# Taking a pacing wait off the slot scatters on GpSimd

## The chip, the cores and the metric

The program runs on 1 core of one Trainium2 chip. The metric is the device time of one execution in microseconds. Before the change it is 4115.81 us, the median of 3 executions (4109.86 to 4130.47).

## The reference

A block of a graph network with three parts. Node features are 6250 x 256, in float32; there are 200,000 edges sorted by target node.

```python
xn = _layernorm(x, axis=-1)
x = x + gnn(xn, ..., src, dst) + linear_attention(xn[None])[0]
x = x + moe(_layernorm(x, axis=-1)[None])[0]
# gnn: gather per edge by src, a small MLP per edge, segment_sum by dst, two linear maps
# moe, for 8 experts of 256 -> 1024 -> 256:
probs = softmax(xt @ Wr + br); top_p, top_idx = top_k(probs, 2)
weights = top_p / top_p.sum()
y = experts(xt)                       # every token
out = (weights * y[top_idx]).sum()    # two experts of 8 per token
```

The kernel computes only the two chosen experts of each token. For that it must sort tokens by expert: each token gets two slots in a table, one in the region of each of its experts.

## The kernel before, in words

The program has stages one after the other. The times are from the start of the profiled execution.

- **Prepare and nodes** (to about 350 us): layer norm, the node tables, attention sums.
- **Edges** (to about 3110 us): per item of four pieces of 128 edges, GpSimd (POOL) issues four indirect gathers (L812), TensorE (PE) computes edge weights (L953, L959), VectorE (DVE) and ScalarE (ACT) build messages, PE sums them by target (L972), and DVE adds the sums to accumulators (L870).
- **Update** (about 3122 to 3395 us), the stage of the change: 49 tiles of 128 tokens.
- **Experts** (from about 3395 us): blocks of 512 or 256 slots. POOL gathers token rows through the slot table and scatters weighted results.

In the update stage a step `s` handles several tiles at once, in a software pipeline. PE turns the sums of tile s+1 (L1200), makes the attention denominators of s+2 and s+1 (L1212, L1216), turns tile s-1 (L1238), makes the output of tile s (L1225, L1229) and the router logits of s-1 (L1244). DVE adds the residual and so completes a tile of `x2` (L1370, `onto_residual`), and computes statistics, shares and denominators (L1355, L1359, L1365). ACT copies results out of PSUM (L1297, L1303, L1310). SyncE (SP) loads residuals and queries three and four tiles ahead and stores tokens. The semaphore `c["x2"]` counts completed tiles.

Routing is done in batches of tiles, `SIZES = [8, 8, 8, 8, 8, 3, 3, 3]`; `done_at[b]` is the step at which batch b is complete. DVE runs one part of it in each of the steps `done_at[b]` to `done_at[b] + 4`: moments, best expert, next expert, weights, places. The first part hands two numbers per token to POOL for a power of -1/2 (`powers`, L1172), and the second waits for it. The last part, `places`, ends in `c["placed"]` (L1446), which says that the slot number of each token of the batch is known.

POOL then writes the slot table. `scatter(b, j)` issues two indirect DMAs (L1181), one for each chosen expert of the 128 tokens of tile j of the batch. Each writes 128 rows of 8 bytes to DRAM. A batch of eight thus has 16 of them. Each `scatter` waits for `placed`, and also for a count of `x2` that goes up by one per j (L1178). POOL's code is written out by a plain loop over steps, so between `scatter(b, 4)` and `scatter(b, 5)` stands `powers(b + 1)`. For batches 5 to 7 the work of several batches is interleaved.

At the end of the stage SP waits until all 98 scatters have landed and then loads the first rows of the slot table for the experts.

Of the kernel before, what the change touches and what calls it, by code (L numbers as in the profile page):

```python
# [21 lines left out]
NT = -(-N_NODES // P)  # L22
# [985 lines left out]
def update(nc, A, K, acc, out):  # L1008

    with ExitStack() as ctx:  # L1010
# [39 lines left out]
        c = {z: m.sem(z) for z in (  # L1050
            "ctxT", "ctxT_copied", "folded", "fold", "columns", "centred", "mid", "turned", "midT", "den", "positive", "inverse", "by_head", "share",
            "out", "x2", "passed", "stats", "x2_turned", "xT", "logits", "raw", "spread", "powers", "runner_up", "exp", "scales",
            "upto", "ranked", "counted", "placed", "known", "tok", "begun", "pads", "pads_out", "made")}
# [6 lines left out]
        done_at = [FIRSTS[b] + SIZES[b] for b in range(NB_R)]  # L1060
# [88 lines left out]
        @block.gpsimd  # L1149
        def _(pool):  # L1150
            g = nc.gpsimd
            g.iota(pads[:, :, 0], [[1, 512]], base=N_PAD, channel_multiplier=0)
            g.memset(pads[:, :, 1], 0).then_inc(c["pads"], 1)
            g.iota(ramp[:, :, :], [[0, MOST], [-1, E]], base=E, channel_multiplier=0, allow_small_or_imprecise_dtypes=True)
            g.iota(rows[:, :, :, 0], [[0, TOP], [P, NT]], base=0, channel_multiplier=1)
            g.iota(hot[0][:, :, 0:1], [[CAP // P, E]], base=0, channel_multiplier=0, allow_small_or_imprecise_dtypes=True)
            g.iota(origin[:, :], [[CAP, E]], base=0, channel_multiplier=0, allow_small_or_imprecise_dtypes=True)
            g.iota(number[:, 0:NDUO], [[1, NDUO]], base=0, channel_multiplier=0, allow_small_or_imprecise_dtypes=True)
            g.iota(number[:, NDUO:NBK], [[1, NSOLO // 2], [0, 2]], base=NDUO, channel_multiplier=0,
                   allow_small_or_imprecise_dtypes=True)  # L1160
            g.iota(number[:, NBK:], [[1, NSOLO]], base=0, channel_multiplier=0, allow_small_or_imprecise_dtypes=True)
            g.iota(ahead[:, 0:NDUO], [[2 * SB, NDUO]], base=0, channel_multiplier=0, allow_small_or_imprecise_dtypes=True)
            g.iota(ahead[:, NDUO:], [[2 * SB, NSOLO // 2], [SB, 2]], base=2 * SB * NDUO, channel_multiplier=0,
                   allow_small_or_imprecise_dtypes=True)
            g.memset(mask[:, :, :], 1.0).then_inc(c["made"], 1)
            pool.wait_ge(c["made"], 1)
            g.memset(mask[:, :, 0:1], 0.0).then_inc(c["made"], 1)
            pool.wait_ge(c["pads_out"], 16)

            def powers(b):  # L1170
                pool.wait_ge(c["spread"], b + 1)
                g.tensor_tensor(power[:, :, of(b)], power[:, :, of(b)],  # L1172
                                K.minus_half[:, 0:size(b)].unsqueeze(1).to_broadcast([P, 2, size(b)]),
                                ALU.pow).then_inc(c["powers"], 1)

            def scatter(b, j):
                pool.wait_ge(c["placed"], b + 1)
                pool.wait_ge(c["x2"], min(done_at[b] + 4 + j, NT))  # L1178
                for i in range(TOP):
                    z = TOP * FIRSTS[b] + i * SIZES[b] + j  # L1180
                    g.indirect_dma_start(out=K.slots_d, out_offset=bass.IndirectOffsetOnAxis(ap=where_i[:, z:z + 1], axis=0),  # L1181
                                         in_=rows[:, i, FIRSTS[b] + j, :], in_offset=None, bounds_check=NROW - 1, oob_is_err=True).then_inc(scattered, 16)

            for s in range(end_step + MOST):
                for b in range(NB_R):
                    if s == done_at[b]:
                        powers(b)
                    if 0 <= s - done_at[b] - 4 < SIZES[b]:
                        scatter(b, s - done_at[b] - 4)
# [767 lines left out]
```

## Time and profile before

| what | value |
|---|---|
| median of 3 executions | 4115.81 us |
| the profiled execution | 4115.81 us |
| its span, first to last instruction | 4114.1 us |
| mean granted TensorE clock | 0.935 of full |
| busy: PE / DVE / ACT / POOL | 85% / 65% / 64% / 57% of the span |

The profiled execution is the median one, and 1.7 us of it lie outside its span. An engine's busy time leaves out its waits. The busy shares are means over stages with different limits, so they say little about the update stage, which is 7% of the span.

### The profile page before, as it was taken

The page shows a single profiled execution, that of the slowest core. Times are in us where ns is not written, and L with a number is a line of the kernel's source. Part 1 is how long each engine was busy: PE and PEld are TensorE (multiplying, and loading weights), DVE is VectorE, ACT ScalarE, POOL GpSimd, SP SyncE. Part 2 cuts the span into 40 slices and gives each one's busy share as a digit, 9 for nine tenths or more (in the row PEclk, how much of TensorE's full clock was granted, in tenths as well). Part 3 has the DMA queues.
Part 4 walks back from the last instruction along what each step waited for, and adds up shares of the span by engine and source line. Part 5 has one row for each costly group of instructions (what it writes and reads, how often), then busy time and mean ns, then how long its engine had stood idle before and what let it go on. Part 6 is the DMA issues. An engine that isn't in the chain of part 4 may idle for free. (4 is left out here: it accounts for less than half of the span.)

```text
span 4114.1 us, 68468 instructions
## 1 busy us (share of the span) xinstructions
PE 3510.4 (85%) x16169; PEld 2945.0 (72%) x16169; DVE 2667.4 (65%) x4940; ACT 2635.5 (64%) x8253; POOL 2355.2 (57%) x2141
## 2 busy tenths in 40 slices
PE   6978888888988888888888888888888958999998
PEld 5867677676766776676676767677667847888887
DVE  7857677666767666676666767667785545565541
ACT  6666676666666666666666766666664536667652
POOL 6646666655656665666666666665641554445442
PEclk9989999999999999999999999999899979999999
DMA  7843233323323333333332333333323654454444
GB/s 233 276 152 88 83 86 89 87 80 84 90 82 90 84 86 82 85 90 85 86 86 82 91 88 85 87 86 84 85 70 91 117 117 125 127 148 126 131 116 131
DMA packets 321360, 431.06 MB, mean 105 GB/s; under 512 B 128875, under 2 KB 249143, under 8 KB 313079
## 3 DMA queue, kind: packets, MB, share of 16 engines
q0 software_dynamic: 105936, 253.72, 23.3%
q1 hardware_dynamic: 215335, 176.28, 14.8%
q8 instruction: 41, 0.67, 0.1%
q14 instruction: 48, 0.39, 0.0%
HBM read 365.18 MB, written 64.59 MB: 104 GB/s over the span
## 5 line engine op out<-in xcount | busy, mean ns | idle before, releaser
L812 POOL DMA_INDIRECT k_x<-gather_table,edges_edge x1612 | 1759.3, 1091 | 1075.9 <-issue 727.4
L831 ACT ACTIVATE k_x<-k_x,edges_edge 128x64 f32<-128x64 f32 x4836 | 1196.5, 334 | 28.9 <-DVE k_x L904 13.5
L959 PE MATMUL edges_ps_edge<-k_w_e,edges_hT 100*128 100x256 f32 x3224 | 851.7, 411 | 309.3 <-issue 155.5
L972 PE MATMUL edges_ps_sum<-k_x,edges_hot_y 128*128 128x256 f32 x3224 | 1003.6, 393 | 127.2 <-issue 75.9
L972 PE MATMUL edges_ps_sum<-k_x 128*128 128x256 f32 x3224 | 985.1, 387 | 11.4 <-issue 11.4
L959 PEld LDWEIGHTS edges_ps_edge<-k_w_e,edges_hT 100*128 100x128 f32 x3224 | 647.6, 205 | 458.5 <-issue 282.6
L841 ACT ACTIVATE edges_hot_y<-k_x,edges_edge 128x128 f32<-128x128 f32 x1612 | 516.7, 390 | 502.6 <-remote 346.8
L972 PEld LDWEIGHTS edges_ps_sum<-k_x,edges_hot_y 128*128 128x128 f32 x3224 | 624.7, 197 | 281.4 <-issue 152.5
L972 PEld LDWEIGHTS edges_ps_sum<-k_x 128*128 128x128 f32 x3224 | 629.9, 195 | 110.1 <-issue 18.5
L870 DVE TENSOR_TENSOR accumulators<-accumulators,edges_ps_sum 128x512 f32 x477 | 325.9, 683 | 431.8 <-remote 338.9
L904 DVE TENSOR_TENSOR k_x<-k_x,edges_ps_edge 128x512 f32<-128x512 f32 x403 | 275.7, 684 | 398.0 <-remote 320.3
L823 ACT ACTIVATE edges_hT<-edges_ps_hidden 100x512 f32<-100x512 f32 x403 | 237.7, 590 | 409.0 <-remote 296.3
L888 DVE TENSOR_TENSOR k_w_kvT<-k_x,edges_edge 128x768 f32<-128x768 f32 x403 | 384.4, 954 | 16.9 <-DMA k_x<-gather_table,edges_edge 16.8
L907 DVE TENSOR_TENSOR k_x<-k_x,edges_ps_edge 128x768 f32<-128x768 f32 x403 | 381.7, 947 | 0.0
L1763 ACT ACTIVATE experts_g<-experts_ps_h,weights_constants 128x512 f32<-128x512 f32 (+1 forms) x256 | 162.8, 638 | 246.5 <-PE experts_ps_h L1690 240.6
L879 DVE SCALAR_TENSOR_TENSOR k_x<-k_iota_f,k_item_base,edges_edge 128x512 f32<-128x512 f32 (+2 forms) x477 | 314.1, 663 | 1.9 <-issue 1.6
L1638 POOL DMA_INDIRECT out<-experts_y,weights_rows x112 | 198.0, 1768 | 167.1 <-issue 87.6
L1800 DVE TENSOR_TENSOR experts_g_lo<-experts_g,experts_g_hi 128x512 fp32r<-128x512 f32 x192 | 132.4, 690 | 227.4 <-ACT experts_g_hi L1763 227.4
L953 PE MATMUL edges_ps_hidden<-edges_el,k_w_e1s 128*100 128x512 f32 x403 | 253.5, 629 | 16.4 <-DMA edges_el<-el_parts 15.9
L1628 POOL DMA_INDIRECT k_x<-tokens,weights_rows x112 | 125.5, 1120 | 239.7 <-DMA weights_rows<-slots 186.7
L898 DVE TENSOR_TENSOR k_x<-k_w_kvT 128x256 f32<-128x256 f32 x403 | 171.1, 425 | 12.1
L894 DVE TENSOR_TENSOR k_w_kvT<-k_w_kvT 128x256 f32<-128x256 f32 x403 | 168.4, 418 | 0.0
(308 smaller groups left out, 4456.1 us busy)
## 6 DMA issues: line engine op xcount, KB each, us to landing
k_x<-in_w SPq DMA_DIRECT2D x64, 1024.0 KB
k_x<-gather_table,edges_edge POOLq DMA_INDIRECT x1612
el_parts<-nodes_el_parts SPq DMA_DIRECT2D x41, 384.0 KB
edges_el<-el_parts SPq DMA_DIRECT2D x355, 40.0 KB
edges_el<-el_parts SPq DMA_DIRECT2D x425, 20.0 KB
nodes_el<-in_el SPq DMA_DIRECT2D x41, 192.0 KB
k_x<-in_x SPq DMA_DIRECT2D x7, 896.0 KB
residual<-nodes_res SPq DMA_DIRECT2D x49, 128.0 KB
```

What stands on the lines that cost most here:

```text
L812: nc.gpsimd.indirect_dma_start(out=rows[k][:, j, :], out_offset=None, in_=K.table_d.rearrange("t p d -> (t p) d"), in_offset=bass.Indirect ...
L823: nc.scalar.activation(hT[k % 2][:, :], ps_h[k % 2][0:HID, :], ACT.Silu, scale=1 / math.sqrt(BAS)).then_inc(c["act"], 1)
L831: x = nc.scalar.activation(g[:, j, D + MUL * (i + 1):D + MUL * (i + 2)], g[:, j, 2 * D:MSG], ACT.Identity, scale=y[k][:, j, 1 + i:2 + i])
L841: x = nc.scalar.activation(hot_y[k % 2][:, j, :], hot[k][:, j, :], ACT.Identity, scale=y[k][:, j, 0:1])
L870: v.tensor_tensor(a, a, ps_s[ph.bank(k, j)][:, :], ALU.add).then_inc(c["flushed"], 1)
L879: v.scalar_tensor_tensor(hot[k][:, at, :], K.iota_f[:, :].unsqueeze(1).to_broadcast([P, ph.len, P]), K.item_base[:, bass.ds(ph.seq(n) + j, ...
L888: v.tensor_tensor(dot3[:, :, :, :], rows[k][:, :, MUL:D].rearrange("p c (i u) -> p c i u", i=3), y[k][:, :, 1:4].unsqueeze(3).to_broadcast ...
L904: v.tensor_tensor(g.rearrange("p c (b u) -> p c b u", u=MUL)[:, :, 0:MSG // MUL:8, :], f[:, :, 0:MUL].unsqueeze(2).to_broadcast([P, GC, 2, ...
L907: v.tensor_tensor(g[:, :, MUL:D].rearrange("p c (i u) -> p c i u", i=3), f[:, :, MUL:D].rearrange("p c (i u) -> p c i u", i=3), w[:, :, 1: ...
L953: t.matmul(ps_h[k % 2][0:HID, :], K.w_e1s[:, :], el[k][:, :], start=True, stop=True).then_inc(c["hidden"], 1)
L959: x = t.matmul(ps_e[k % 2][:, j * 256:(j + 1) * 256], hT[k % 2][:, j * P:(j + 1) * P], K.w_e2[:, :], start=True, stop=True)
L972: x = t.matmul(into[:, :, o, :], rows_hot[:, j, :], msg[k % 2][:, j, o * D:(o + 1) * D], start=j % ph.len == 0 and o == 0, stop=(j + 1) % ...
```

## The change

One wait is deleted from `scatter`. After it, a scatter waits for `placed` of its batch alone.

```diff
             def scatter(b, j):
                 pool.wait_ge(c["placed"], b + 1)
-                pool.wait_ge(c["x2"], min(done_at[b] + 4 + j, NT))
                 for i in range(TOP):
                     z = TOP * FIRSTS[b] + i * SIZES[b] + j
                     g.indirect_dma_start(out=K.slots_d, ...)
```

No instruction is added, removed or moved on any engine. POOL's queue at the end of batch 0 and the start of batch 1, before the change, from the first of the last two `scatter` calls ahead of `powers(1)`. In the brackets, `nodes_el_out1` is the hardware semaphore that this stage uses again as `x2`:

```order
L1181 DMA slots<-update_rows,update_where_i 65536x2 [waits nodes_el_out1,update_placed]
L1181 DMA slots<-update_rows,update_where_i 65536x2
L1181 DMA slots<-update_rows,update_where_i 65536x2 [waits nodes_el_out1,update_placed]
L1181 DMA slots<-update_rows,update_where_i 65536x2
L1172 TENSOR_TENSOR update_power<-update_power,k_minus_half 128x2x8 [waits update_spread]
```

The same place after the change:

```order
L1180 DMA slots<-update_rows,update_where_i 65536x2 [waits update_placed]
L1180 DMA slots<-update_rows,update_where_i 65536x2
L1180 DMA slots<-update_rows,update_where_i 65536x2 [waits update_placed]
L1180 DMA slots<-update_rows,update_where_i 65536x2
L1172 TENSOR_TENSOR update_power<-update_power,k_minus_half 128x2x8 [waits update_spread]
```

Only the wait is gone. Ten scatters still stand ahead of the next batch's powers, and six behind it.

## Rows read from the trace of the kernel before

**Rows 1.** Busy time by stretch (start:end, length, five engines, clock, DMA share, GB/s).
```profile
3122.00:3182.00 60.00, 55.22 (x413) 52.28 (x413) 26.61 (x113) 29.95 (x63) 5.45 (x14) 0.94 0.40 121
3182.00:3329.00 147.00, 136.23 (x994) 129.49 (x995) 75.78 (x336) 82.53 (x172) 76.16 (x69) 0.92 0.61 119
```

**Rows 2.** Waits in 3182 to 3329 us (total, times, longest).
```profile
POOL slots L1181 <- DVE k_x L1370: 35.9, 16, 4.8
...
DVE k_x L1370 <- DMA el_parts<-nodes_el_parts: 15.9, 4, 4.0
```

**Rows 3.** The scatters as a group, same stretch (busy us, mean ns, idle before).
```profile
L1181 POOL DMA_INDIRECT slots<-update_rows,update_where_i x64 | 63.1, 986 | 77.5 <-DVE k_x L1370 35.9 <-DVE update_where_i L1446 26.5 <-issue 15.1
```

**Rows 4.** DVE in order of time, before any scatter (start, duration, [idle before]).
```profile
3158.59 0.42 DVE L1370 TENSOR_TENSOR k_x<-update_ps_out,k_w_nodeA 128x256 f32<-128x256 f32 x1 [1.38 <-PE update_ps_out L1229]
3162.30 0.42 DVE L1370 TENSOR_TENSOR k_x<-update_ps_out,k_w_nodeB 128x256 f32<-128x256 f32 x1 [1.38 <-PE update_ps_out L1229]
```

**Rows 5.** POOL in order of time, the scatters of batch 0.
```profile
3182.41 1.09 POOL L1181 DMA_INDIRECT slots<-update_rows,update_where_i  x1 [13.78 <-DVE update_where_i L1446]
...
3186.39 0.98 POOL L1181 DMA_INDIRECT slots<-update_rows,update_where_i  x1 [0.30 <-issue]
3189.71 0.98 POOL L1181 DMA_INDIRECT slots<-update_rows,update_where_i  x1 [2.35 <-DVE k_x L1370]
...
3198.66 2.93 POOL L1172 TENSOR_TENSOR update_power<-update_power,k_minus_half 128x16 f32<-128x16 f32 x1
```

**Rows 6.** DVE in order of time, around the first and the fourth batch's first scatters.
```profile
3182.14 0.42 DVE L1370 TENSOR_TENSOR k_x<-update_ps_out,update_resid 128x256 f32 x1 [0.61 <-PE update_ps_out L1229]
...
3188.43 0.42 DVE L1370 TENSOR_TENSOR k_x<-update_ps_out,update_resid 128x256 f32 x1 [4.04 <-DMA el_parts<-nodes_el_parts]
...
3191.62 0.42 DVE L1370 TENSOR_TENSOR k_x<-update_ps_out,k_w_nodeA 128x256 f32 x1 [1.60 <-PE update_ps_out L1229]
...
3298.26 0.42 DVE L1370 TENSOR_TENSOR k_x<-update_ps_out,update_resid 128x256 f32 x1 [3.94 <-DMA el_parts<-nodes_el_parts]
```

**Rows 7.** PE and ACT in order of time, within batch 0's first scatters.
```profile
3185.88 0.63 PE L1200 MATMUL update_ps_mid<-k_ident,update_mid 128*128 128x128 f32 x4
...
3188.37 0.58 ACT L1297 COPY update_midT<-update_ps_mid 128x512 f32<-128x512 f32 x1 [2.17 <-DMA nodes_dst<-in_dst_rows,first_groups_i]
```

**Rows 8.** Waits in 3182 to 3329 us, those at DVE's L1355 between pairs.
```profile
DVE update_den L1355 <- DMA nodes_dst<-in_dst_rows,first_groups_i: 4.8, 2, 2.4
```

**Rows 9.** The edges stage in order of time: two runs of eight gathers.
```profile
2916.91 1.01 POOL L812 DMA_INDIRECT k_x<-gather_table,edges_edge  x1 [2.19 <-DMA edges_el<-el_parts]
...
2921.53 0.59 PE L953 MATMUL edges_ps_hidden<-edges_el,k_w_e1s 128*100 128x512 f32 x1
...
2926.11 1.01 POOL L812 DMA_INDIRECT k_x<-gather_table,edges_edge  x1 [0.30 <-issue]
...
2928.51 0.69 DVE L904 TENSOR_TENSOR k_x<-k_x,edges_ps_edge 128x512 f32<-128x512 f32 x1 [6.60 <-remote]
...
2940.23 1.01 POOL L812 DMA_INDIRECT k_x<-gather_table,edges_edge  x1 [0.30 <-issue]
...
2949.19 0.69 DVE L870 TENSOR_TENSOR accumulators<-accumulators,edges_ps_sum 128x512 f32 x1 [4.56 <-remote]
```

**Rows 10.** The tail of the update stage: runs of six and of ten scatters.
```profile
3329.14 1.04 POOL L1181 DMA_INDIRECT slots<-update_rows,update_where_i  x1 [4.14 <-DVE update_where_i L1446]
...
3336.34 0.17 DVE L1355 TENSOR_SCALAR update_den<-update_ps_den 128x8 f32<-128x8 f32 x1 [3.63 <-DMA nodes_dst<-in_dst_rows,first_groups_i]
...
3344.49 0.98 POOL L1181 DMA_INDIRECT slots<-update_rows,update_where_i  x1 [2.38 <-DVE update_where_i L1446]
...
3351.76 0.17 DVE L1374 COPY update_raw<-update_ps_turned 128x8 f32<-128x8 f32 x1 [2.40 <-remote]
```

**Rows 11.** Busy time by stretch, the second and the third batch's scatters.
```profile
3217.00:3253.00 36.00, 33.00 (x249) 31.22 (x250) 18.45 (x81) 20.60 (x43) 18.91 (x18) 0.95 0.66 116
3253.00:3292.00 39.00, 36.63 (x242) 34.70 (x240) 17.83 (x79) 19.91 (x42) 18.46 (x17) 0.82 0.61 107
```

## The prediction

> **What bounds the kernel now.** I read the busy time by stretch first, then the waits of the update stage, then POOL, DVE, PE and ACT there in order of time. Everything the change touches lies between 3182 us, when the first batch is placed, and about 3395 us. In 3182 to 3329 us PE is busy 136.23 of 147 us, DVE 75.78 and POOL 76.16 [rows 1]. So the stretch follows the loop PE to DVE to PE, with PE nearly full, and POOL is half idle. POOL's idle time in itself is worth nothing. In 60 us without scatters PE was about as full, and a tile took 3162.30 - 3158.59 = 3.71 us with a regular DVE wait of 1.38 us for PE's output [rows 1, 4]. That is the pace to measure by.
>
> **What the deleted wait does now.** It holds POOL 16 times, for 35.9 us together [rows 2], so it does bind. Over four batches of eight tiles there are 64 scatters of 0.986 us [rows 3]. When batch 0 is placed, the count of `x2` is already high enough for the first two tiles, so four scatters go back to back, 3182.41 to 3187.37; the gap between two is 0.3 us, so 1.29 us each. After that they go in pairs, each pair released by one more tile of `x2` (the next at 3189.71 after 2.35 us of waiting) [rows 5].
>
> **What goes with scatters issued back to back.** This is the step on which the forecast rests. Just within the run of four, DVE's L1370 waits 4.04 us instead of 1.38, and the tile takes 3188.43 - 3182.14 = 6.29 us instead of 3.71 [rows 4, 6]. It ends 1.1 us after the last scatter of the run. The waits show four such cases, one per batch, 15.9 us together [rows 2], the last of them 3.94 us [rows 6]. The page names a DMA as the releaser, and the residual load would be a candidate. But ACT's L1297, whose code waits only for PE, is let go at the same moment, 3188.37, though PE had started the matmuls it waits for at 3185.88, with 0.63 us of work [rows 7]. So what comes late is PE's word that it is finished. The price of a run of four is 15.9/4 - 1.38 = 2.6 us.
>
> The same appears where POOL issues for longer. In the edges stage eight gathers run from 2916.91 to 2927.12. PE starts L953 and the L959 before it by 2921.5, and DVE gets the latter's result only at 2928.51, after 6.60 us, again just behind the end of the run. Another run of eight goes with a wait of 4.56 us [rows 9]. In the tail of the update, where the change alters nothing, six scatters from 3329.14 go with 3.63 us of DVE waiting, and ten from 3344.49 with 2.40 us [rows 10]. Pairs mostly go free, but twice in the four batches DVE waits at L1355, 4.8 us together, between pairs that follow each other closely [rows 8].
>
> **The change part by part.** It removes one wait from 49 `scatter` calls. No instruction, DMA or queue position changes. Without it, the 16 scatters of each of batches 0 to 3 come as ten back to back (10 x 1.29 = 12.9 us), then `powers` of the next batch, which waits for its tiles as before, then six (7.7 us). From batch 4 on POOL issues scatters almost without pause already and the deleted counts have been reached or are reached first; I cost that part at nothing, and if it moved, it would be by the 2 us waits that remain there.
>
> Per batch, the costs are:
>
> - the run of ten: between 2.40 us (the run of ten of the tail) and 6.60 us (a run of eight) [rows 9, 10]. Scaled by length the second would be 6.60 x 10/8 = 8.3. I take 4.5, the middle of 2.40, 4.56 and 6.60, three rows that disagree;
> - the run of six: the one row says 3.63, less an ordinary half microsecond at that line, so 3.1; the lower end is nothing, since what is behind `powers` falls into steps where DVE has routing to do and PE's lateness may be hidden;
> - what goes away: the run of four, 2.6 us, and the waits between pairs, 4.8/4 = 1.2 us;
> - a hold leaves work queued, so the tile behind it is quicker: 3191.62 - 3188.43 = 3.2 against 3.7 us, 0.5 back [rows 6]. There are two holds for one, so 0.5 us more is given back.
>
> Sum: 4.5 + 3.1 - 2.6 - 1.2 - 0.5 = +3.3 us, four batches: +13 us. A gain from `powers` is too small to count: it starts at 3198.66 with no idle time before it, right behind a scatter that the wait had put there [rows 5], and DVE has other work meanwhile; at most 0.2 us a batch. Nor is there a gain at the stage's end. The tail begins when batch 4 is placed (3329.14), and that is DVE's doing [rows 10].
>
> The profiled execution's 4115.8 us is the median; 4115.8 + 13 = **4129 us**.
>
> The Trainium skill (SBUF — State Buffer, Who interferes with whom) says that PE and ACT never wait on anyone, and that only VectorE and GpSimd share a port. By that rule long runs of POOL's DMAs would cost PE nothing, and the sum would be zero. PE's starts in this trace agree with it; its late completions do not. That result is the third rival below.
>
> **The rivals.**
>
> - *Charged by the run.* A run costs 2.6 us whatever its length, because one backlog is cleared at its end. For it: the run of ten in the tail shows 2.40. Against it: 6.60 and 4.56 at eight. Two runs for one and the pairs' 1.2 us: +1.4 x 4 = +6 us, 4121 us.
> - *PE's word is held for as long as the run lasts.* From the third scatter to 1.1 us behind the end, as in the run of four: 12.9 - 2.6 + 1.1 = 11.4 us, 10 above the ordinary wait; for six 6.2, or 4.8 above. 14.8 - 3.8 = +11 us a batch, +44 us, 4160 us. For it: the 6.60 us. Against it: the tail's runs let results through in between.
> - *No hold by POOL at all.* The four cases of 4 us come from something else at the same step of each batch, such as the residual load that the page names. Then nothing changes: 4116 us. Against it: ACT was let go at the same moment [rows 7], and the edges have no residual load.
> - *Faster.* The wait keeps scatters in every step of a batch, and small holds spread through it cost more than two large ones. The place is the pairs (1.2 us a batch), and the third batch took 39 us against 36 with a granted clock of 0.82 against 0.95 [rows 11]: PE at 1.2 in place of 2.4 GHz for part of it. If POOL's quiet half batches keep the clock up, 3 us for one or two batches come back, and the long run must cost no more than the four did: -5 - 6 = -11 us, 4105 us. It decides if a run of ten holds PE under about 3 us.
>
> That the wait doesn't bind I leave out; 16 waits say that it does.
>
> **How the numbers follow.** Forecast 0.50, by the run 0.18, held throughout 0.14, no hold 0.10, faster 0.08. The bounds of the forecast: low 2.4 + 0 - 3.8 = -1.4 a batch, -6 us; high 8.3 + 3.6 - 3.8 = +8 a batch, +32 us, and 12 more if each batch takes the low clock's 3 us. The range of 4108 to 4155 us leaves out most of the second and the last rival. The forecast's own range is 4116 to 4148. A measurement of this kernel can tell about 0.5%, or 20.6 us, from no change. Slower by more takes the second rival's 0.14 and about a third of the forecast's 0.50: 0.31. Faster by more than 0.5% is the far end of the last rival: 0.04. Within 0.5%: 0.65.
>
> **What would show it.** POOL should show runs of ten and six for batches 0 to 3, and no wait of L1181 (L1180 then) for `x2`. Right: within the run of ten DVE or ACT waits 4 to 7 us for a PE result that PE started long before, batches take 37 to 42 us, and the experts start some 13 us later. Wrong: runs of ten with waits near 2.5 us (by the run); waits of 10 us (held throughout); the four waits of 4 us at the same place and of the same length (no hold); or a granted clock that differs over the stage by enough to outweigh the holds.

## The result

The change makes the kernel slower, by more than forecast.

| | before | after |
|---|---|---|
| median | 4112.84 us (4 runs, 4071.93 to 4130.47) | 4164.05 us (4 runs, 4129.53 to 4211.89) |
| ratio, 95% interval | | 1.013, 1.0087 to 1.0172 |
| profiled execution | 4115.8 us | 4183.4 us |
| update stage, residual add of tile 12 to that of tile 48 | 164.7 us | 215.0 us |

The forecast was 4129 us with a range to 4155. The loss is +51.2 us of median instead of +13. The last line of the table is the measure for everything below: the distance between two starts of DVE's residual add (L1370 before, L1369 after, since one line is gone), from where batch 0 is placed to the last tile. It grew by 50.3 us. The profiled execution lost 67.6 us, because its stage also came 19.5 us later (3201.62 against 3182.14 us); no instruction ahead of the stage differs, so that part is not put down to the change.

Busy time by stretch of the kernel after: the stretch before any scatter, and the whole stage measure, with the ends rounded. Columns as in [rows 1].

```profile
3142.00:3201.60 59.60, 55.38 (x414) 52.44 (x415) 26.50 (x112) 30.08 (x63) 5.46 (x14) 0.94 0.39 122
3201.60:3416.60 215.00, 166.21 (x1086) 156.36 (x1085) 88.47 (x393) 89.99 (x189) 87.46 (x80) 0.84 0.38 90
```

The same stretch of the kernel before, in whole:

```profile
3182.14:3346.79 164.65, 150.16 (x1086) 142.62 (x1085) 86.93 (x393) 89.83 (x189) 87.44 (x80) 0.92 0.59 117
```

The first row answers to the first of [rows 1] and is nearly the same. In the others the instructions on PE are as many (1086), and two things grew. PE's busy time rose by 16.05 us, since the mean granted clock fell from 0.92 to 0.84. The records know two levels, 2.4 GHz and 1.2 GHz, so about a third of the stage ran at the lower one (0.16/0.5), against a sixth before. And the time in which PE was not busy rose from 14.5 to 48.8 us, by 34.3. Together that is the 50.3 us. GpSimd (POOL) is as busy as before.

POOL in order of time, kernel after, batch 0. It answers to [rows 5].

```profile
3201.89 1.09 POOL L1180 DMA_INDIRECT slots<-update_rows,update_where_i  x1 [13.77 <-DVE update_where_i L1445]
3203.28 0.98 POOL L1180 DMA_INDIRECT slots<-update_rows,update_where_i  x1 [0.31 <-issue]
...
3213.56 0.98 POOL L1180 DMA_INDIRECT slots<-update_rows,update_where_i  x1 [0.30 <-issue]
3228.84 2.93 POOL L1172 TENSOR_TENSOR update_power<-update_power,k_minus_half 128x16 f32<-128x16 f32 x1 [14.30 <-DVE update_power L1392]
3231.96 1.04 POOL L1180 DMA_INDIRECT slots<-update_rows,update_where_i  x1 [0.19 <-issue]
...
3238.45 0.98 POOL L1180 DMA_INDIRECT slots<-update_rows,update_where_i  x1 [0.30 <-issue]
```

The runs of ten and six are there. After its ten POOL now waits 14.30 us for DVE with `powers`; before it came to `powers` with no idle time. All that the deleted wait cost POOL came back as another wait.

What else happens in those ten scatters, PE first, then ACT, then DVE:

```profile
3205.36 0.64 PE L1199 MATMUL update_ps_mid<-k_ident,update_mid 128*128 128x128 f32 x4
...
3206.20 0.69 PE L1215 MATMUL update_ps_den<-k_ident,update_by_head 128*128 128x128 f32 x4
```
```profile
3212.05 0.58 ACT L1296 COPY update_midT<-update_ps_mid 128x512 f32<-128x512 f32 x1 [6.40 <-DMA nodes_dst<-in_dst_rows,first_groups_i]
```
```profile
3207.88 0.42 DVE L1369 TENSOR_TENSOR k_x<-update_ps_out,update_resid 128x256 f32 x1 [4.04 <-DMA el_parts<-nodes_el_parts]
...
3216.35 0.17 DVE L1354 TENSOR_SCALAR update_den<-update_ps_den 128x8 f32<-128x8 f32 x1 [5.10 <-DMA nodes_dst<-in_dst_rows,first_groups_i]
...
3217.10 0.42 DVE L1369 TENSOR_TENSOR k_x<-update_ps_out,k_w_nodeA 128x256 f32 x1
...
3225.18 0.42 DVE L1369 TENSOR_TENSOR k_x<-update_ps_out,k_w_nodeB 128x256 f32 x1 [3.12 <-PE update_ps_out L1228]
```

PE had done L1199 by 3206.0 us, and ACT gets it at 3212.05. PE had done L1215 by 3206.9 us (ends on PE are modelled), and DVE gets it at 3216.35, which is 9.5 us later and 1.8 us behind the end of the last scatter (3214.54). DVE had been free to take it for the last 5.10 us of these. The DMAs that are named as releasers belong to the start of the program and have long landed. Tiles 13, 14 and 15 take 6.26, 9.22 and 8.08 us; 3.71 is the pace of [rows 4]. Busy time by tile, the same columns:

```profile
3201.62:3207.88 6.26, 5.27 (x44) 4.97 (x43) 1.54 (x7) 2.70 (x6) 4.77 (x5) 1.00 0.47 76
3207.88:3217.10 9.22, 2.14 (x14) 1.90 (x14) 1.63 (x7) 0.69 (x2) 5.14 (x6) 0.85 0.30 38
3217.10:3225.18 8.08, 7.45 (x34) 7.09 (x35) 1.63 (x7) 4.06 (x9) 0.00 (x0) 0.53 0.23 69
```

The run of ten covers tiles 13 and 14 alone. In tile 14 PE is idle for 7.1 of 9.22 us. Tile 15 begins behind the run: there POOL does nothing and PE is idle for 0.6 us, but the granted clock is 0.53, so PE works almost wholly at 1.2 GHz. The hold costs tiles 13 and 14, and the low clock that follows costs tile 15.

### The profile page after: what moved, and what is told of

Its sections match the earlier page's. It is cut to its first block and busy times, and to the rows that moved or that the text cites. A ratio compares the mean times of both kernels' runs of the same rounds, so it can differ in the third digit from the quotient of the medians.

```text
span 4181.7 us, 68419 instructions
## 1 busy us (share of the span) xinstructions
PE 3539.5 (85%) x16169; PEld 2965.8 (71%) x16169; DVE 2671.1 (64%) x4940; ACT 2638.9 (63%) x8253; POOL 2351.8 (56%) x2141
## 3 DMA queue, kind: packets, MB, share of 16 engines
q0 software_dynamic: 105936, 253.72, 22.7%
## 5 line engine op out<-in xcount | busy, mean ns | idle before, releaser
L959 PE MATMUL edges_ps_edge<-k_w_e,edges_hT 100*128 100x256 f32 x3224 | 861.1, 414 | 343.1 <-ACT edges_hT L823 179.8
L1637 POOL DMA_INDIRECT out<-experts_y,weights_rows x112 | 198.4, 1771 | 164.9 <-issue 98.9
L953 PE MATMUL edges_ps_hidden<-edges_el,k_w_e1s 128*100 128x512 f32 x403 | 257.8, 640 | 19.5 <-DMA edges_el<-el_parts 19.5
```

Source lines behind the costliest of these rows:

```text
L959: x = t.matmul(ps_e[k % 2][:, j * 256:(j + 1) * 256], hT[k % 2][:, j * P:(j + 1) * P], K.w_e2[:, :], start=True, stop=True)
```

## The experiments

All of them use the stage measure of above. "PE idle" is its length less PE's busy time. e3 to e9, e14 and e15 are single executions, and executions of the kernel before spread over 50 to 75 us on a chip, so of these only the stage is read. It is one profile each, but it comes back well: 215.0 and 208.4 us for after, 142.3 and 143.4 for pairs, 142.2 and 142.1 without writes.

| kernel | stage us | PE busy | PE idle | clock | median, and the kernel before on that chip |
|---|---|---|---|---|---|
| before | 164.7 | 150.2 | 14.5 | 0.92 | 4112.8 |
| after | 215.0 | 166.2 | 48.8 | 0.84 | 4164.1 / 4112.8 |
| e1 pairs | 142.3 | 137.6 | 4.7 | 0.99 | 4047.3 / 4062.9 |
| e2 singles | 162.0 | 152.3 | 9.6 | 0.89 | 4057.7 / 4062.9 |
| e3 fours | 174.0 | 150.1 | 23.9 | 0.93 | 4078.5 / 4062.9 |
| e4 no writes | 142.2 | 137.6 | 4.6 | 0.99 | 4030.7 / 4062.9 |
| e5 compute instead | 146.4 | 139.4 | 7.0 | 0.98 | 4058.2 / 4087.5 |
| e6 gathers instead | 210.6 | 164.9 | 45.7 | 0.83 | 4098.5 / 4087.5 |
| e7 direct writes by POOL | 182.1 | 162.9 | 19.1 | 0.84 | 4072.0 / 4087.5 |
| e8 direct writes by SP | 192.9 | 155.8 | 37.1 | 0.86 | 4081.9 / 4087.5 |
| e9 spaced, other chip | 155.8 | 146.4 | 9.4 | 0.94 | 3562.1 / 3554.5 |
| e10 after, other chip | 149.0 | 139.4 | 9.5 | 0.99 | 3552.5 / 3554.5 |
| e11 pairs, other chip | 146.6 | 138.5 | 8.1 | 0.99 | 3552.5 / 3554.5 |
| e12 after again | 208.4 | 164.2 | 44.2 | 0.84 | 4110.7 / 4059.9 |
| e13 pairs again | 143.4 | 136.4 | 7.0 | 1.00 | 4052.8 / 4059.9 |
| e14 spaced again | 180.0 | 161.4 | 18.7 | 0.87 | 4075.3 / 4059.9 |
| e15 no writes again | 142.1 | 137.6 | 4.6 | 0.99 | 4028.3 / 4059.9 |

### How long may a run be: e1, e2, e3

The **pairs** kernel starts each batch's scatters a step later and waits for one more tile of `x2`, so that the first count is not yet reached when the batch is placed.

```diff
-                pool.wait_ge(c["x2"], min(done_at[b] + 4 + j, NT))
+                pool.wait_ge(c["x2"], min(done_at[b] + 5 + j, NT))
...
-                    if 0 <= s - done_at[b] - 4 < SIZES[b]:
-                        scatter(b, s - done_at[b] - 4)
+                    if 0 <= s - done_at[b] - 5 < SIZES[b]:
+                        scatter(b, s - done_at[b] - 5)
```

> Every scatter one step later, gated one x2 count later: so no run is longer than two (before: one run of four per batch). The stage's measure is the time from DVE's L1370 of tile 12 to that of tile 48: 164.7 us before, 215.0 after. Theory (PE's results are held while POOL issues software DMAs without pause, the more the longer the run): the four waits of 4 us at L1370 go, about 2.1 us each, so some 8 us less than before, 156 us; whole kernel 0.2% faster. Rival 1 (a price per run, whatever its length): the same number of runs or more, no gain. Rival 2 (something else at that step, such as the residual load): the four waits stay at tiles 13, 21, 29, 37, 165 us.

Measured: 4047.27 us, ratio 0.997 (0.9938 to 1.0001), and a stage of 142.3 us, 14 shorter than expected. POOL in order of time:

```profile
3117.51 0.98 POOL L1181 DMA_INDIRECT slots<-update_rows,update_where_i  x1 [1.25 <-DVE k_x L1370]
3118.79 0.98 POOL L1181 DMA_INDIRECT slots<-update_rows,update_where_i  x1 [0.30 <-issue]
3121.57 0.98 POOL L1181 DMA_INDIRECT slots<-update_rows,update_where_i  x1 [1.80 <-DVE k_x L1370]
```

and DVE's residual adds beside it:

```profile
3112.52 0.42 DVE L1370 TENSOR_TENSOR k_x<-update_ps_out,update_resid 128x256 f32 x1 [0.60 <-PE update_ps_out L1229]
3116.23 0.42 DVE L1370 TENSOR_TENSOR k_x<-update_ps_out,update_resid 128x256 f32 x1 [1.48 <-issue]
3120.29 0.42 DVE L1370 TENSOR_TENSOR k_x<-update_ps_out,k_w_nodeA 128x256 f32 x1 [1.84 <-PE update_ps_out L1229]
3123.64 0.43 DVE L1370 TENSOR_TENSOR k_x<-update_ps_out,k_w_nodeB 128x256 f32 x1 [1.49 <-issue]
```

Tiles 13, 14 and 15 take 3.71, 4.06 and 3.35 us. The 64 scatters of these batches cost nothing when they come two per tile. The wait of 4.04 us within a run of four that [rows 6] shows is gone.

**Singles** puts a further wait (for ACT's `xT`) between the two scatters of a pair.

```diff
                 for i in range(TOP):
+                    if i:
+                        pool.wait_ge(c["xT"], min(done_at[b] + 5 + j, NT))
```

> As e1, and the second scatter of a pair waits for ACT's copy of the same tile (about 1.9 us after x2): no two scatters back to back. Theory: the small holds between pairs (4.8 us in two of the four batches) go as well: 150 to 156 us for tiles 12 to 48. Rival 1 (price per run): twice as many runs as e1, slower than e1 by up to 2 us per tile. Rival 2: as before, 165 us.

Measured: 4057.73 us, ratio 0.9981 (0.9947 to 1.0015), stage 162.0 us. A miss: the added wait also stands ahead of `powers` of the next batch. DVE waited 7.8 us for `powers` in four waits, and the clock was 0.89. It says nothing of single scatters.

**Fours** releases two `scatter` calls by one count.

```diff
-                pool.wait_ge(c["x2"], min(done_at[b] + 4 + j, NT))
+                pool.wait_ge(c["x2"], min(done_at[b] + 4 + j // 2 * 2, NT))
```

> The gate opens for two tiles at a time: runs of four every two tiles (three whole ones a batch, and one split by the powers). Theory: each costs what the run of four of before costs (2.6 us of waiting less 0.5 us given back), two more per batch less the pairs' 1.2 us: +3 us a batch, 177 us for tiles 12 to 48, between before and after. Rival 1 (price per run): the same number here. Rival 2: 165 us. If runs of four spread out cost no more than pairs, the price begins only beyond a fixed length.

Measured: 4078.46 us in one run, stage 174.0 us (expected 177). PE's idle time is 23.9 us against 14.5 before and 4.7 with pairs. By run length the PE idle of the stage goes 4.7 (twos), 14.5 (a four per batch), 23.9 (fours) and 48.8 us (tens and sixes); 3 to 4 us of each of the last three lie in tiles 45 to 48.

### What in a scatter does it: e4 to e8

These start from the kernel after and leave out the slot writes of the update stage, or put something else in their place; what the experts then read is not the reference's table. e4 and e5 also leave out SP's wait for the scatters at the end, so their medians don't compare with the others. One line of the cut belongs to each run, as its comment says.

```diff
-                    g.indirect_dma_start(out=K.slots_d, ...).then_inc(scattered, 16)
+                    pass                                                    # e4
+                    g.memset(pads, 0).then_inc(filled, 1)                   # e5, 128 x 1024, behind the one before
+                    g.indirect_dma_start(out=pads[:, z, :], in_=K.slots_d, ...)   # e6, reads 128 rows of 8 bytes
+                    g.dma_start(K.junk_d[z], rows[:, i, ...])               # e7, direct write, same bytes
```

> The slot writes of the update stage are left out (the experts then read an empty table), all else as after. It gives the floor of the stage: 36 tiles of 3.70 us are 133 us, routing adds some 1.3 us per batch and the low clock some: 140 to 150 us for tiles 12 to 48 by the theory, and no wait of L1370 of 4 us. Rival 2 (not POOL's DMAs): the four waits stay and the stage takes 160 us or more.

Measured: stage 142.2 us, the same as with pairs. This is the floor.

> As after, with each scatter replaced by a memset of 128x1024 words on POOL (about 1.1 us), so POOL is as busy, at the same places, with no DMA; the slot writes are left out. Tiles 12 to 48 take 142.2 us without any scatter, 142.3 with pairs, 215.0 with the runs of ten and six of after. If POOL's work as such (its port, its power) holds PE's results, 180 us or more; if it is its DMAs, 142 to 146 us.

Measured: stage 146.4 us, and no hold. POOL was nearly as busy (84.8 us) as with scatters (87.5). That POOL is busy, and writes to SBUF, is not the cause.

> As after, with each scatter replaced by an indirect gather of the same 128 rows of 8 bytes out of the slot table into SBUF; the slot writes are left out. If the issue of software DMAs holds PE's results, the same as after, 200 to 215 us for tiles 12 to 48; if the small writes to DRAM do it, about 142 to 150 us.

Measured: stage 210.6 us, with a clock of 0.83. The waits of the stage, kernel after and then e6 (total, times, longest):

```profile
ACT update_midT L1296 <- DMA nodes_dst<-in_dst_rows,first_groups_i: 35.1, 5, 10.6
DVE update_den L1354 <- DMA nodes_dst<-in_dst_rows,first_groups_i: 30.3, 9, 5.1
...
DVE k_x L1369 <- DMA el_parts<-nodes_el_parts: 23.1, 5, 6.9
```
```profile
ACT update_midT L1296 <- DMA nodes_dst<-in_dst_rows,first_groups_i: 31.8, 6, 7.6
DVE update_den L1354 <- DMA nodes_dst<-in_dst_rows,first_groups_i: 29.7, 9, 5.1
DVE k_x L1369 <- DMA el_parts<-nodes_el_parts: 21.9, 9, 5.3
```

So the direction of the transfer and writing to DRAM matter little (210.6 against 215.0 and 208.4 us). Indirect DMAs that POOL issues one behind the other do it: as much busy time of POOL is in e5 too, and without loss.

> As after, with each scatter replaced by a direct write of 128 rows of 8 bytes from the same tile to a scratch tensor in DRAM, issued by POOL; the slot writes are left out. If the issue holds PE, it follows POOL's time per DMA: with about 1 us each again 200 to 215 us; if only indirect DMAs do it, 142 to 150 us.

Measured: stage 182.1 us, but not for the same reason. A direct DMA held POOL 0.54 us instead of 0.99, and DVE's longest wait for PE at the residual add was 2.3 us (here with PE's wait for its next queries, which the stage before never had):

```profile
DVE k_x L1368 <- PE update_ps_out L1227: 28.8, 20, 2.3
PE update_ps_den L1210 <- DMA update_qT<-queries_T: 17.4, 9, 4.4
```

POOL's ten in batch 0:

```profile
3128.89 5.43 POOL L1180 DMA_DIRECT2D junk<-update_rows  x10 [13.20 <-DVE update_where_i L1444]
```

Tiles 13, 14 and 15 take 3.70, 4.06 and 3.35 us here, the same as in e1 (in the other batches the three take 11.1, 12.2 and 11.1 us, against 11.1 in e1). Ten direct DMAs on end, 5.4 us in all, held nothing. Four indirect ones of 5.0 us in all did in the kernel before [rows 5, 6]. What slows this stage comes elsewhere: tiles 20, 24, 36 and 40 take 7.6 to 10.1 us, and tiles 45 to 48 take 24.4 us at a clock of 0.57.

**e8** lets SP issue the 16 direct writes of a batch back to back, and POOL none:

```diff
+                b = batch(4)
+                if b is not None:
+                    for z in range(TOP * FIRSTS[b], TOP * done_at[b]):
+                        sp.dma_start(K.junk_d[z], K.ones[:, 0:2].bitcast(i32)).then_inc(scattered, 16)
```

> As after, with the scatters of a batch replaced by as many direct writes of 128 rows of 8 bytes to DRAM, issued back to back by SP at the step of the places, so the DMA engines do the writes but POOL issues nothing; SP's loop is written out; the slot writes are left out. If the writes or their completions hold PE's results, 160 us or more with waits at the tiles behind the places; if POOL's issue does it, 142 to 150 us, unless SP's own loads of queries come late behind 16 writes.

Measured: stage 192.9 us; one tile per batch took 12 to 17 us, each behind this wait of PE:

```profile
PE update_ps_den L1216 <- DMA update_qT<-queries_T: 31.2, 4, 11.1
```

SP spent 8.5 us on issuing the writes and came late to the load of the queries. So e7 and e8 slow the stage mostly on another path, late queries. Where that path is not in play, in tiles 13 to 15 of e7, small direct writes by POOL hold nothing. What part of an indirect DMA does it they don't show, and a run of direct ones as long in time as the run of ten indirect ones (12.7 us) was not tried.

### Another chip: e9, e10, e11

**Spaced** is the kernel after with a short piece of work behind each pair of scatters.

```diff
+                if b < 4:
+                    if fills[0]:
+                        pool.wait_ge(filled, fills[0])
+                    fills[0] += 1
+                    g.memset(pads[:, 0:256, :], 0).then_inc(filled, 1)
```

> The changed kernel (runs of ten and six), with a memset of 512 columns on GpSimd (about 0.5 us, sized from the 0.95 us of 1024 columns measured in e5_fill) behind each pair of scatters of batches 0 to 3. No wait for x2; the pairs are merely spaced, one about every 3.5 us instead of every 2.6. Theory (the reports of PE come late while GpSimd issues one indirect DMA after another, and a pause as long as one tile's loop gives them back): tiles within the run take under 5 us and the stage from tile 12 to tile 48 about 150 to 165 us. Rival (the hold lasts as long as indirect DMAs are issued with less than one free tile between them, whatever short pauses there are): tiles of 6 to 9 us and a stage of 200 us or more, as after the change (215).

> The changed kernel once more, beside the pairs on the same chip. Theory (holds of 10 us a batch, plus the low clock that follows from PE's waiting): stage from tile 12 to tile 48 205 to 220 us with 60 to 75 us at the lower clock, and the time 1.0 to 1.7% above the kernel before. Rival (the 50 us of the stage were largely this one execution's clock): stage under 195 us, low clock under 45 us, and a ratio to before under 1.008.

> The pairs kernel of e1_pairs once more (every scatter call one tile of x2 later than before the change, so that two scatters per tile are issued and no run is longer). Theory: stage 142 to 150 us, no DVE wait over 2.5 us at the residual add, time 0.3 to 0.8% under the kernel before and 1.5 to 2.2% under the changed one. Rival (its 142 us were a lucky clock): stage 155 us or more and a ratio of 1.00.

These three met a chip on which the kernel before took 3554.5 us instead of 4060 to 4113 (25 of 28 executions here lie within 3528 to 3565 us, three near 3480). After and pairs took 3552.5 us both, spaced 3562.1 in one run. There is no interval for these ratios. But there is no loss to see, and the stage of the changed kernel took 149.0 us. It issues the same run of ten, here POOL and then ACT:

```profile
2639.40 1.09 POOL L1180 DMA_INDIRECT slots<-update_rows,update_where_i  x1 [13.78 <-DVE update_where_i L1445]
...
2651.07 0.98 POOL L1180 DMA_INDIRECT slots<-update_rows,update_where_i  x1 [0.30 <-issue]
```
```profile
2643.54 0.58 ACT L1296 COPY update_midT<-update_ps_mid 128x512 f32<-128x512 f32 x1 [0.38 <-PE update_ps_mid L1199]
2647.24 0.58 ACT L1296 COPY update_midT<-update_ps_mid 128x512 f32<-128x512 f32 x1 [0.38 <-PE update_ps_mid L1199]
2650.95 0.58 ACT L1296 COPY update_midT<-update_ps_mid 128x512 f32<-128x512 f32 x1 [0.38 <-PE update_ps_mid L1199]
```

ACT is served every 3.7 us after 0.38 us of waiting, where it waited 6.40 us above. POOL issues at the same pace; only PE's results aren't held. (The expectation of e12 counts semaphore records of PE that come over 0.5 us late. Such a count is no measure: pairs have 56 of 184, and lose nothing, against 57 in the kernel after. What counts is the waits of ACT and DVE.) The edges stage shows the same difference for the same code. Busy time from 400 to 2500 us, first the kernel after as first compared, then e10:

```profile
400.00:2500.00 2100.00, 1769.85 (x7464) 1465.83 (x7463) 1427.20 (x2389) 1403.32 (x5077) 1305.16 (x1195) 0.93 0.31 85
```
```profile
400.00:2500.00 2100.00, 2074.10 (x9313) 1737.48 (x9311) 1802.87 (x3069) 1764.19 (x6332) 1634.53 (x1491) 1.00 0.39 106
```

In the same 2100 us the second chip got through 9313 matmul instructions instead of 7464, with PE busy 99% of the time. So the program has two regimes, and late results of PE go with the slower one, as far as one chip of the faster kind can tell. What makes a chip the one or the other the traces do not show. None of the three expectations could be decided on it, so the kernels were run once more.

### The first kind of chip again: e12 to e15

> The changed kernel a third time. On the chip of e9 to e11 the kernel before took 3554.5 us, no report of PE came more than 0.5 us late in the update stage (1 of 183) and the change cost nothing there (stage 149.0 us). If this chip is of the other kind (the kernel before at 4050 to 4120 us, dozens of late reports), theory: stage 200 to 220 us, ratio to before 1.008 to 1.017. If it is of the fast kind: stage 145 to 152 us and a ratio of 1.00. Rival (the 50 us of the first comparison were one execution's clock, on any chip): a chip of the slow kind with a stage under 185 us and a ratio under 1.005.

Measured: 4110.74 us against 4059.88, ratio 1.0122 (1.0088 to 1.0156), stage 208.4 us. The loss of +50.9 us is repeated.

> Pairs only (every scatter call one tile of x2 later than before the change), beside e12. On a chip of the slow kind: stage 142 to 150 us, time 0.2 to 0.7% under the kernel before and 1.2 to 2.2% under the changed one. On a chip of the fast kind: as before and after within 0.3%. Rival: stage 155 us or more on a chip of the slow kind.

Measured: 4052.79 us, ratio 0.9984 (0.9954 to 1.0015), stage 143.4 us: 1.4% under e12 (4110.74/4052.79). Against the kernel before, pairs are not shown to be faster: both intervals hold 1.000, though the stage is 21 to 22 us shorter than in the one profile of before.

> e9 once more: runs of ten and six with a memset of about 0.5 us behind each pair, since on the fast kind of chip there was nothing to tell apart. On a chip of the slow kind, theory (a short pause behind each pair gives PE's reports back): stage 145 to 165 us. Rival (short pauses don't help, the reports wait until indirect DMAs stop for about a tile): 200 us or more. On a chip of the fast kind it tells nothing.

Measured: 4075.28 us in one run, stage 180.0 us. Neither side: pauses of about 0.5 us behind each pair take PE's idle time from 44.2 to 18.7 us, but the clock stays low (0.87). Spacing by time helps by about half; spacing by tile, as in e13, helps wholly.

> The slot writes of the update stage left out (as e4_none). It gives the floor of this chip for the stage from tile 12 to tile 48, by which e12 to e14 are measured: 142 us on either kind of chip if only GpSimd's indirect DMAs make PE's reports late; over 150 us on a chip of the slow kind if something else does too.

Measured: stage 142.1 us. Without indirect DMAs by POOL, this chip's floor is that of e4.

## Why the prediction was wrong

- **That the deleted wait binds, and runs of ten and six follow:** right.
- **That PE's results come late to DVE and ACT while POOL issues:** right on this kind of chip, and on it the rest depends. e4, e5 and e6 show that issuing indirect DMAs, not POOL's being busy nor the direction of the transfer, brings it about. The rival *no hold by POOL at all* is refuted for this kind of chip.
- **The price of what goes away (run of four 2.6 us, pairs 1.2 us, 0.5 us given back, 4.3 in all):** too high. The first tile in the run of four is 6.29 - 3.70 = 2.6 us longer than in e1, as said. But the tile behind it is 0.9 us shorter, and the waits between pairs come in two batches only. PE's idle time in the four batches is 7.0 us over that of e4, or 1.75 a batch; the other 2.9 us over the floor lie in tiles 45 to 48. Pairs cost nothing in e1 and e13. The two waits of [rows 8] were between pairs that caught up behind a run of four; that this is their cause was not tried alone.
- **The run of ten at 4.5 us: the failed step.** It was sized by one wait of one engine per run. But each tile that falls within the run is held anew. PE's idle time in tiles 13 to 15 and their like is 8.7, 7.0, 7.1 and 6.8 us in the four batches, and nothing in e1: 7.4 us a batch instead of 4.5. With the low clock that follows, the three tiles take 12 us more than in e1 (22.7 to 23.6 instead of 11.1). The run of ten of [rows 10], which pulled the value down with its 2.40, counted one wait of one engine too.
- **The run of six at 3.1 us:** right. PE's idle time in tiles 16 to 20 and their like is 3.0 us a batch over that of e4. With the low clock they take about 5 us more.
- **The clock, given 3 us per batch in the upper bound and nothing in the sum: the other half of the failure.** PE's busy time grew by 16.0 of the 50.3 us, 4.0 a batch. With PE stalled the granted clock fell, to 0.53 in tile 15. It doesn't follow the stalls in proportion (e14: PE idle 18.7 us, clock 0.87; before: 14.5 and 0.92), so its size stays a reading and not a rule.
- **The sum:** per batch +2.9 for the run of ten, +4.0 for the clock and about +2.5 for what goes away are the 9.3 us between the forecast's +3.3 and the measured +12.6.
- **That the part from batch 4 on is worth nothing, and `powers` too:** right; tiles 45 to 48 take 19.1 instead of 18.6 us.
- **The rival *held for as long as the run lasts*:** it priced +11 us a batch and 4160 us. Measured are +50.3/4 = +12.6 a batch and a median of 4164 us. That is partly luck. Its hold of 11 us a batch measured (48.8 - 14.5)/4 = 8.6, and the clock, which it left out, made up the rest. Nor is its picture right as it stands. DVE's first wait, 4.04 us, ended just behind the run of four before [rows 5, 6], and the prediction read the run's end as what freed it. After the change the same wait of 4.04 us ends at the same place (3207.88), with five scatters still to come in the run, and ACT gets its result at 3212.05, also within it. So results do come through during a run, but late.
- **The rival *faster*, by a quieter half batch that keeps the clock up:** refuted; the low clock grew from a sixth to a third of the stage.

The rule of the Trainium skill (SBUF — State Buffer, Who interferes with whom) that PE and ACT never wait on anyone gives the right time on the chip of e9 to e11 (no loss) and the wrong one on the others (+50 us). PE's starts agree with it on both. On the others PE's results don't, though the section speaks of SBUF's ports, and no run here shows that a port is where they are held.

What stays open: why the chips differ, which part of POOL's issue of an indirect DMA does the holding, and whether PE's matmuls end late or only the word of it, since the profile records their starts and models their ends.

## What to carry over

A pacing wait on an engine that is half idle may be there for its neighbours. Before taking it off, ask how many of its instructions will then stand in a row, and price each tile that falls within the row, not only the first stall, and then the low clock behind it. On the slower kind of chip two indirect DMAs per tile of work were free in this kernel, four in a row cost about 2 us, ten in a row about 12 us, of which 7.4 were PE standing idle.

Measure such a thing on more than one chip: the same two kernels differed by 1.2 to 1.3% in two comparisons and by nothing that could be seen in a third, on another chip.

## What was not expected of the hardware

- Executions of one kernel had medians of 4060 to 4113 us on some chips and 3554 us on another. Most of the difference lies in the stage where POOL issues indirect gathers all the time (in 2100 us 1195 gathers against 1491).
- The result of a matmul group was taken 9.5 us after its modelled end, 1.8 us behind the end of POOL's last indirect DMA, by an engine that had stood waiting for it for 5.10 us. PE itself had meanwhile gone on with work that was ready (14 matmul instructions in tile 14).
- The profile put such waits down to DMAs that had long landed (`nodes_dst`, `el_parts`). The sign that it is not that DMA: two engines that wait for different results of PE are let go in the same moment, as DVE and ACT in [rows 6, 7].
